# Joining the block scaling, moving the snapshot and q's transposes, and splitting the attention products in a linear-attention + FP4 block

## What is computed

```
xn = layernorm(x)
out = x + attention(xn) + ffn(xn)

attention:  q, k, v = split(xn @ W_qkv.T)        # 16 heads of 16
            q = softmax(q over the head's 16) / 4 ; k = exp(k)
            # tokens in buckets of 64; a bucket sees the sums of the buckets before it
            ksum    = exclusive cumsum over buckets of sum(k)
            context = exclusive cumsum over buckets of k^T v
            attn = (q context) / max(q . ksum, 1e-6)
            return attn @ W_out.T

ffn:        fp4_linear(a, w) = fq(a) @ fq(w).T
            # fq: blocks of 16 along the last dim, scale = max(|block|) / 6 (at least 1e-12),
            # each value to the nearest of 0, .5, 1, 1.5, 2, 3, 4, 6 times its scale
            h = silu(fp4_linear(xn, w_gate)) * fp4_linear(xn, w_up)      # 704 wide
            return fp4_linear(h, w_down)
```

## Time and profile before

| | |
|---|---|
| median of 3 runs | 1361.32 us (1359.19 to 1363.07) |
| the profiled execution | 1361.72 us, its span 1360.0 us |
| ACT busy | 969.4 us, 71% |
| POOL busy | 355.0 us, 26% |
| instructions | 41012 |
| granted TensorE clock, mean | 0.989 |
| HBM | 19.99 MB read, 16.78 MB written, 27 GB/s |

### The profile page before, as it was taken

One profiled execution on the slowest core, in us unless ns is written; L12 is line 12 of the kernel. 1 busy time (PEld: TensorE's weight loads), 2 busy tenths in 40 slices (PEclk: granted clock), 3 DMA queues, 4 the chain that ended last, 5 costly groups with the idle time before them and its releaser, 6 DMA issues.

```text
span 1360.0 us, 41012 instructions
## 1 busy us (share of the span) xinstructions
PE 1271.1 (93%) x9934; PEld 871.0 (64%) x9934; DVE 1309.7 (96%) x3901; ACT 969.4 (71%) x3221; POOL 355.0 (26%) x791
## 2 busy tenths in 40 slices
PE   0279999999999999999999999999999999999996
PEld 0157666666666666666666666666666666666664
DVE  6869999999999999999999999999999999999996
ACT  1567777777777777777777777777777777777772
POOL 2212223222222323222222222223232222323220
PEclk9889999999999999999999999999999999999998
DMA  4024544444454444444544444545454454445444
GB/s 129 12 40 82 108 98 100 105 100 102 98 114 100 101 105 98 103 100 98 113 101 105 98 102 99 112 98 104 105 109 99 92 115 101 96 105 110 97 83 91
DMA packets 432380, 133.64 MB, mean 98 GB/s; under 512 B 397404, under 2 KB 431836, under 8 KB 432348
## 3 DMA queue, kind: packets, MB, share of 16 engines
q1 hardware_dynamic: 431622, 132.60, 46.8%
q10 hardware_dynamic: 726, 0.72, 0.2%
HBM read 19.99 MB, written 16.78 MB: 27 GB/s over the span
## 4 chain that ended last, share of the span: by engine, by line
DVE 52%; issue 33%; DVEq 7%; PE 5%; ACT 2%; DMA 1%; SPq 0%; ACTq 0%
DVE hx_v L880 7%; DVE ga L810 5%; DVE blk L834 3%; DVE xring L963 3%; DVE hx_v L887 3%; DVE h L820 2%; DVE drec L794 2%; DVE xq_s L935 2%; DVE q_rows L922 2%; DVE att L799 2%; DVE osum L958 2%; DVE blk L843 1%; DVE dz L786 1%; DVE hrow L854 1%; DVE dmx L790 1%
## 5 line engine op out<-in xcount | busy, mean ns | idle before, releaser
L418 POOL TENSOR_TENSOR xn_s<-xn,xn_s 128x256 f16<-128x256 f32 x128 | 108.6, 848 | 820.3 <-ACT xn_s L535 820.3
L1165 PE MATMUL outp<-w_down_cat,q_rows 128*128 128x256 f16 x1408 | 246.1, 274 | 0.0
L617 ACT ACTIVATE snap<-ctxp,mask 64x68 f32<-64x68 f32 x1024 | 236.5, 310 | 3.3
L1165 PEld LDWEIGHTS outp<-w_down_cat,q_rows 128*128 128x128 f16 x1408 | 138.3, 98 | 16.5
L1167 PE MATMUL outp<-w_down_lo,q_rows 128*128 128x256 f16 x640 | 147.6, 274 | 0.0
L580 ACT ACTIVATE th<-unit0a,c_g 128x352 f32<-128x352 f32 x128 | 71.0, 554 | 97.3 <-PE unit0b L1078 95.3
L556 ACT ACTIVATE qexp<-qsh,c_q 128x256 f32<-128x256 f32 x128 | 65.1, 508 | 99.0 <-DVE qsh L773 98.8
L580 ACT ACTIVATE th<-unit1a,c_g 128x352 f32<-128x352 f32 x128 | 71.0, 555 | 87.4 <-PE unit1b L1078 65.0
L827 DVE TENSOR_REDUCE blk<-h 128x44 f32<-128x704 f32 x128 | 123.8, 967 | 0.1
L411 POOL TENSOR_TENSOR att_s<-att,att_s 128x256 f16<-128x256 f32 x128 | 87.9, 687 | 108.1 <-ACT att_s L572 108.1
L880 DVE TENSOR_TENSOR hx_v<-h,blk 128x704 f32<-128x704 f32 x128 | 111.0, 868 | 0.0
(11 more groups left out here) (199 smaller groups left out, 4059.0 us busy)
## 6 DMA issues: line engine op xcount, KB each, us to landing
xring<-x SPq DMA_DIRECT2D x128, 128.0 KB, 2.7
out<-xring SPq DMA_DIRECT2D x128, 128.0 KB, 2.5
xnt<-xn_s SPq DMA_TRANSPOSE x128, 2.5
xqt<-xq_s SPq DMA_TRANSPOSE x128, 2.4
att_t<-att_s SPq DMA_TRANSPOSE x128, 2.5
q_rows<-q_rows SPq DMA_TRANSPOSE x128, 3.6
raw_qkv<-wqkv_t SPq DMA_DIRECT2D x1, 768.0 KB, 4.4
raw_up<-wup ACTq DMA_DIRECT2D x2, 352.0 KB
```

The costliest lines, as they stand in the source:

```text
L418: nc.gpsimd.tensor_tensor(xn_s[:, par, 1, :], xn[:, par, :], xn_s[:, par, 0, :], ALU.subtract).then_inc(xn_lo, 1)
L617: nc.scalar.activation(kept[:, :, cols], sums[:, :, cols], ACT.Copy, scale=mask[rows, f, h:h + 1])\
L1165: nc.tensor.matmul(downp, hqt[:, par, m, :], w_down_cat[:, m, :], start=(m == 0), stop=False)
```

## The change

1. **Joined block scaling.** `block_scales` makes one instruction, `blk * SIX_TIE * 2^11` and the maximum with a tile `blk_floor` (60 columns, set once ahead of the loop), for h's 44 and x's 16 blocks. It waits for both maxima. A semaphore `blk_scaled` takes the place of one count each in `xq_step` (6 to 5 per tile) and `hq_step` (9 to 8).
2. **Snapshot between the tanh.** ACT runs `snapshot(k + 1)` right behind the first `tanh_gate`, and not as the last of the step. `squares_wait` stands ahead of `high_xn`, and `copy_qt` becomes ACT's last operation of the step.
3. **q's transposes last.** PE runs `transpose_q(k + 1)` at the end of the step, with a new wait for `att_step` of the tile before, that is for `attention(k)` of the same step to be over.
4. **Numerators.** Eight products of 64 rows of contraction and 72 columns, in place of four of 128 and 144. The halves `f` go to two banks: `nump` and `trp` are now the two halves of one tensor `pair`, and the numerators of `f = 1` lie in the bank of q's transposes, beside them.
5. **DVE's attention.** Reads go over both banks by one access pattern; the factor 4e-6 moves from the second part to the first; the product is two instructions of 128 elements, one for each `f`; it stands before `gate_h` of the second half, right behind the reciprocal.

The diff, cut to its core (counts of `xq_step` and `hq_step` that only shift are left out):

```
+        blk_floor = sb("blk_floor", [P, FB + XB])
...
-        nump = pb("nump")
+        pair = ctx.enter_context(nc.psum_tensor("pair", [P, 1024], fp32))
+        nump = pair[:, 0:512]
-        trp = pb("trp")
+        trp = pair[:, 512:1024]
+        nums = pair[:, :].rearrange("p (f x) -> p f x", f=2)[:, :, 2 * P:2 * P + HG * SW].rearrange("p f (g c) -> p g f c", c=SW)
...
                 tanh_gate(k, 0, par)
+                snapshot(k + 1)
                 normalise_waits(k + 3)
                 mean_waits(n, d + 4)
                 tanh_gate(k, 1, par)
                 factor_of_row(k - 1, odd)
                 normalise(n, d + 3)
                 mean_of(n, d + 4)
+                squares_wait(k + 4)
                 high_xn(k + 3, odd)
-                squares_wait(k + 4)
+                squares_of(n, d + 4)
                 copy_qt(k + 1, odd)
-                squares_of(n, d + 4)
-                snapshot(k + 1)
...
-                    nc.vector.tensor_copy(dz[:, :, :], num[:, :, CW:SW]).then_inc(att_step, 1)
+                    nc.vector.tensor_scalar(dz[:, :, :].rearrange("p (g f) h -> p g f h", f=2), nums[:, :, :, CW:SW], 4e-6, None, ALU.mult).then_inc(att_step, 1)
...
-                    nc.vector.scalar_tensor_tensor(dmx[:, :, :], dz[:, :, :], 4e-6, num[:, :, HD:CW:HE], ALU.mult,
-                                                   ALU.max).then_inc(att_step, 1)
+                    nc.vector.tensor_tensor(dmx[:, :, :].rearrange("p (g f) h -> p g f h", f=2),
+                                            dz[:, :, :].rearrange("p (g f) h -> p g f h", f=2),
+                                            nums[:, :, :, HD:CW:HE], ALU.max).then_inc(att_step, 1)
...
+                    for f in range(2):
+                        end = nc.vector.tensor_tensor(att[:, par, :].rearrange("p (g f h e) -> p f g h e", f=2, h=HH, e=HD)[:, f],
+                                                      nums[:, :, f, 0:CW].rearrange("p g (h e) -> p g h e", e=HE)[:, :, :, 0:HD],
+                                                      drec[:, :, :].rearrange("p (g f) (h o) -> p f g h o", f=2, o=1)[:, f]
+                                                      .broadcast_to([P, HG, HH, HD]), ALU.mult)
+                    end.then_inc(att_step, 1)
...
             def block_scales(t, u):
-                if is_tile(u):
-                    dve.wait_ge(xq_step, after(u, 6, 1))
-                    nc.vector.tensor_scalar(xblk[:, 1, :], xblk[:, 0, :], SIX_TIE * 2.0 ** 11, XS * TINY * 2.0 ** 11, ALU.mult, ALU.max)\
-                        .then_inc(xq_step, 1)
-                if is_tile(t):
-                    dve.wait_ge(hq_step, after(t, 9, 1))
-                    nc.vector.tensor_scalar(hblk[:, 1, :], hblk[:, 0, :], SIX_TIE * 2.0 ** 11, h_floor[:, :], ALU.mult, ALU.max)\
-                        .then_inc(hq_step, 1)
+                do_h, do_x = is_tile(t), is_tile(u)
+                if do_h:
+                    dve.wait_ge(hq_step, after(t, 8, 1))
+                if do_x:
+                    dve.wait_ge(xq_step, after(u, 5, 1))
+                if do_h or do_x:
+                    both = slice(0 if do_h else FB, FB + XB if do_x else FB)
+                    nc.vector.scalar_tensor_tensor(blk[:, 1, both], blk[:, 0, both], SIX_TIE * 2.0 ** 11, blk_floor[:, both],
+                                                   ALU.mult, ALU.max).then_inc(blk_scaled, 1)
...
                 attention(k, par, 2)
+                attention(k, par, 3)
                 gate_h(k, 1, par)
-                attention(k, par, 3)
                 times_up(k, 1, par)
...
                 pe.wait_ge(q_exp, after(t))
                 if begun(t - 1):
+                    pe.wait_ge(att_step, after(t - 1, 4))
+                if begun(t - 1):
                     pe.wait_ge(qt_done, after(t - 1))
...
+                pe.sem_inc(num_turn, 1)
                 for g in range(HG):
                     for s in range(2):
-                        rows = slice(s * BUCKET, (s + 1) * BUCKET)
-                        last = nc.tensor.matmul(nump[rows, g * 2 * SW:(g + 1) * 2 * SW],
-                                                qt[:, par, g * P + s * BUCKET:g * P + (s + 1) * BUCKET],
-                                                snap[:, g, s, :, :].rearrange("p f c -> p (f c)"), start=True, stop=True)
+                        for f in range(2):
+                            rows, cols = slice(s * BUCKET, (s + 1) * BUCKET), slice(f * VW, (f + 1) * VW)
+                            at = f * 512 + 2 * P + g * SW
+                            last = nc.tensor.matmul(pair[rows, at:at + SW],
+                                                    qt[cols, par, g * P + s * BUCKET:g * P + (s + 1) * BUCKET],
+                                                    snap[cols, g, s, f, :], start=True, stop=True)
...
                 gate_up(k, 1, par)
-                transpose_q(k + 1, odd)
                 project_att(k - 2, par)
                 project_h(k - 2, par)
+                transpose_q(k + 1, odd)
```

More of the change, by code:

```diff
@@ L203, in linear_attention_fp4_ffn_block @@
         num_done = sem("num_done")
+        num_turn = sem("num_turn")
         att_step = sem("att_step")
@@ L295, in turn_xq @@
                     return
-                sp.wait_ge(xq_step, after(t, 6))
+                sp.wait_ge(xq_step, after(t, 5))
                 sp.sem_inc(sp_turn, 1)
@@ L306, in turn_h @@
                     return
-                sp.wait_ge(hq_step, after(t, 9))
+                sp.wait_ge(hq_step, after(t, 8))
                 sp.sem_inc(sp_turn, 1)
@@ L520, in normalise_waits @@
                 if begun(t - 2):
-                    act.wait_ge(xq_step, after(t - 2, 6, 3))
+                    act.wait_ge(xq_step, after(t - 2, 5, 2))
             def normalise(n, d):
@@ L585, in scales_x @@
                     return
-                act.wait_ge(xq_step, after(t, 6, 2))
+                act.wait_ge(blk_scaled, t + 1)
                 nc.scalar.activation(xs_hi[:, :].rearrange("p (b i) -> p b i", i=2), twice(xblk[:, 1, :]), ACT.Copy)\
@@ L592, in factor_of_row @@
                     return
-                act.wait_ge(hq_step, after(t, 9, 4))
+                act.wait_ge(hq_step, after(t, 8, 3))
                 if begun(t - 2):
@@ L600, in scales_h @@
                     return
-                act.wait_ge(hq_step, after(t, 9, 5))
+                act.wait_ge(hq_step, after(t, 8, 4))
                 nc.scalar.activation(hs_hi[:, :].rearrange("p (b i) -> p b i", i=2), twice(hblk[:, 1, :]), ACT.Copy,
@@ L818, in times_up @@
                 if begun(t - 2):
-                    dve.wait_ge(hq_step, after(t - 2, 9, 6))
+                    dve.wait_ge(hq_step, after(t - 2, 8, 5))
                 nc.vector.tensor_tensor(h[:, par, half * FH:(half + 1) * FH], ga[:, half, :],
@@ L852, in over_one @@
                 if do_h:
-                    dve.wait_ge(hq_step, after(t, 9, 2))
+                    dve.wait_ge(blk_scaled, t + 4)
                     nc.vector.tensor_reduce(hrow[:, 0, :], hblk[:, 1, :], AX.X, ALU.max).then_inc(hq_step, 1)
@@ L856, in over_one @@
                     if do_x:
-                        dve.wait_ge(xq_step, after(u, 6, 2))
+                        dve.wait_ge(blk_scaled, u + 1)
                     both = slice(0 if do_h else FB, FB + XB if do_x else FB)
@@ L862, in row_scale @@
                 if is_tile(t):
-                    dve.wait_ge(hq_step, after(t, 9, 3))
+                    dve.wait_ge(hq_step, after(t, 8, 2))
                     if begun(t - 1):
@@ L871, in over_row @@
                     return
-                dve.wait_ge(hq_step, after(t, 9, 4))
+                dve.wait_ge(hq_step, after(t, 8, 3))
                 nc.vector.reciprocal(hrow[:, 2, :], hrow[:, 1, :]).then_inc(hq_step, 1)
@@ L920, in scale_h @@
                 else:
-                    dve.wait_ge(hq_step, after(t, 9, 7))
+                    dve.wait_ge(hq_step, after(t, 8, 6))
                 nc.vector.tensor_tensor(rows(hq_s[:, par, part * F:(part + 1) * F]), rows(hx_q[:, 0:F].bitcast(fp16)),
@@ L929, in scale_x @@
                 dve.wait_ge(hx_step, hx_after(t, 3))
-                dve.wait_ge(xq_step, after(t, 6, 4))
+                dve.wait_ge(xq_step, after(t, 5, 3))
                 if begun(t - 2):
@@ L1051, in _ @@
             low_cols()
-            dve.wait_ge(factors, 11)
+            dve.wait_ge(factors, 13)
             for n in range(0, 2):
```

17 lines of the change are left out of this document (8 added, 9 removed).

## The result

The changed kernel takes 1402.54 us (median of 5 runs, 1401.23 to 1403.29), the kernel before 1360.36 on the same chip (1359.19 to 1363.07): 1.0304 times the time, 95% interval 1.0291 to 1.0317. Over 120 steps of the middle a step grew from 9.907 to 10.248 us; 120 times 0.341 is 40.9 us, near the 39.9 us by which the span grew (1360.0 to 1399.9).

The account below looks back on a forecast made before the run. The prediction took a loop through PE, ACT, POOL and DVE as the bound; two steps of 19.65 + N, N = 0.7, give 10.18 us a step, +0.30 over some 121 steps, +36 on 1361.7: 1398 us, range 1366 to 1420.

Parts of the forecast that it names:

- the loop through ACT and POOL: PE's products release ACT's tanh, ACT releases POOL, whose subtraction holds DVE's scaling: 10.18 us a step, +0.30; chance 0.56.
- DVE's own list: DVE's work in a step without holds: 9.68 + 0.24 + 0.06 - 0.02 = 9.96 us.
- The bound of the kernel before: A loop through all engines at 9.885 us a step; DVE's own work 9.68, PE without waits 9.75.
- Begins at the same place: The joined scaling starts where L847 did, behind L827's end; unblocked it saves 0.02 us, and POOL can hold it.
- DVE's order: Product behind reciprocal, times_up behind gate_h: two back-to-back dependences, +0.24 us a step, and +0.06 for the split product.
- N: Length of PE's numerators stage with sixteen instructions: taken as 0.7 us, bounds 0.4 (half the columns' time) to 1.06.
- A: Start of the first half of DVE's attention product L799, from which the loop's times are counted.
- rival 1: POOL is through before DVE's scaling asks; DVE's own work sets 9.96 us a step, 1371 us; chance 0.18.
- the long scaling: Sign on DVE: the joined scaling's mean well above 0.25 us, its ends coinciding with those of POOL's L411.
- None ahead of the output projection: Sign on PE: idle ahead of the transposes on the attention product, but none ahead of L1074's output projection.
- rival 2: Products of different rows run beside each other (N = 0.4) and chained DVE instructions cost nothing: 1346 us; chance 0.11.
- Rival 3: PE's new products cost time: N above 1.06, PE sets the step with 9.30 + N; at 1.25, 1442 us; chance 0.06.

Follow-up runs that it names:

- The first experiment: The changed kernel with the two waits ahead of the joined scaling exchanged, x's maximum first and h's last: 1390.11 us, ratio 1.0207 to the kernel before.

## Why the prediction was right, and where it wasn't

The forecast was 1398 us, the range 1366 to 1420, and the time 1402.5. The number is good, but what I named as the pace isn't it: two misses cancelled, and that they did is luck. The forecast had the loop through ACT and POOL at 10.18 a step and DVE's own list at 9.96 behind it. The loop came out lower, some 10.03, and DVE's list higher, 10.25, and the step is the higher of the two.

**The bound of the kernel before** was read rightly. DVE's own 9.68 showed as 9.682 once POOL's work was taken away. PE's 9.75 was no floor, since its transposes' stage gave 0.07 back: in the kernel before that stage is 0.44 in the mean and 0.22 at least, so the 0.29 of the step that I read held 0.07 of waiting.

**The joined scaling.** "Begins at the same place" failed, by 0.11: L834 to L855 is 1.110, where it was L827 to L843 0.884 and some 0.11 to L847. The rows of the dependence were of an instruction with one wait; the new one has two, the late one first. The first experiment shows it, and so do two more kernels: 1.106 with the joined scaling alone, 0.998 with x's wait first and the snapshot moved. What I said of the rest holds: the joined form can be held by POOL as L847 was (392 ns with the old order in the changed kernel, 347 where the snapshot's move is the only other part), as the Trainium skill (SBUF — State Buffer, "Who interferes with whom") has it.

**DVE's order** was +0.30 forecast and is +0.358. Both new dependences have the price taken from the earlier trace rows: the reciprocal to the product is 0.277 for 0.163 to what stood there before, L817 to L827 0.544 for 0.43. The two halves take 0.406 for the forecast 0.40 (0.33 before; that is +0.07, where the sum had +0.06). The 0.05 that I missed is L817's length: behind the reciprocal it took 0.46 (0.377 to the next start, plus 0.08), and in its new place 0.51, as the other `gate_h` of a step always did. The Trainium skill (VectorE: DVE Perf Modes, "The DRAIN you can't avoid") has a chain of copies with a semaphore behind each take no longer than one without. If that meant that a wait for the instruction in front is free, 0.277 for 0.163 says that here it isn't.

**The loop's turn** wasn't in the sum at all: +0.108. Before, times_up overlapped the instruction in front, and with the turn it took 0.54 to the next start for 0.43 without. Now it is 0.75 for 0.44. That the branch is what costs is shown by the kernel with half the turns; that it costs more because times_up itself starts late, as it waits for `ga`, is argued. The kernel before with the order alone has the same 0.75, so it comes from the order.

DVE's list by these: 9.96 + 0.11 + 0.06 + 0.108 = 10.24, measured 10.25.

**The products.** N is 0.41, the end of my bounds that I hadn't taken (half the columns' time, 0.4): sixteen products at 0.026 us each. As a term of the loop that is 0.29 too much in two steps, 0.15 a step; at N = 0.41 the loop gives 10.03, 1379 us. The context's stage grew by 0.05. No run has the new products alone, so this is read from the trace; with DVE's list as the pace, what they save PE doesn't show in the time.

**The loop through ACT and POOL** was followed well. With A = 738.57, gate_up is at A + 3.89 (forecast 3.93 with this N), L416 ends 5.02 behind the second tanh (5.03) and at A + 13.26 (13.39). From the A of the next step, where the projection begins 0.3 later behind the transposes, gate_up is at A + 4.22 and L416 ends at A + 13.61; the mean of the two is 0.04 above the forecast. It doesn't set the pace because DVE asks later: at A + 13.66 in either step, where the unheld DVE of the forecast, at A + 9.96 + 3.06 = A + 13.02, would have been there ahead of both ends, and held. This is rival 1, POOL through before the scaling asks, at a price that my own list, 9.96, had too low; its condition came about mainly by DVE being 0.64 late, and less by POOL being early (0.25 ahead of the 13.68 that N = 0.7 gave). The two limits lie close together: with the waits exchanged, at 10.14 a step, L416 ends 0.12 to 0.13 behind the scaling's start in every other step and doesn't hold it yet; at 0.28, in the old order of the changed kernel, it does (0.36 for 0.22). And with that old order the loop is the pace, at the same 10.25.

**Of what would show it**: L805 0.285 and twice, the second tanh directly behind the snapshot, POOL's small operations directly followed by L416 (740.57 and 740.72), PE waiting ahead of the transposes: all there. Not there are the long scaling and its ends together with those of POOL's subtraction. L817 and L827 are 0.54 apart, not 0.50. The scaling's mean is 229 ns, which I had named as the sign of rival 1. "None ahead of the output projection" failed: PE still waits there for L971, 119 times.

**Rivals 2 and 3.** The first half of rival 2 has its number, N = 0.41 for 0.4, the second failed: the dependences cost what the rows said. The 0.41 agrees with what the Trainium skill says of different tiles, that they work in parallel (TensorEngine Tiling, "Key Properties"); that this is the reason no run here shows. Rival 3 fell with N. In the working PE alone is 9.30 + N in one place and 9.35 + N in another; nothing hangs on it.

## What to carry to other kernels

When an instruction gets a second wait, put the wait that is met last also last in the program: here the other order cost 0.11 us a step. Write down for each new dependence between neighbours of a full engine what it costs (0.11 here), and look at what stands behind the last instruction of a loop. Where POOL and DVE hold each other, an edit of 0.1 us can decide which of them is held, so a single part, right in itself, can cost more than all of them together: time the parts in the combination that you mean to keep.

## What the runs showed that I had not expected

- Two waits ahead of one DVE instruction: 0.147 us behind the end of its input with the late one first, 0.035 with it last.
- Sixteen fp32 instructions of 64 rows, 64 columns of weights and 72 columns take 0.41 us; the eight of 128 rows and 144 columns took 0.54.
- With POOL's subtraction recorded 0.03 us ahead of DVE's instruction of two inputs, POOL is the one held (1.08 for 0.67 us); 0.08 and 0.09 ahead, DVE is (0.96 for 0.52). Between 0.05 and 0.06 the kernel before has both. Taking these holds away gains 27 us of 1361.
- A record of the joined scaling that overlaps the end of POOL's by 0.12 us is no longer than others (0.22 us); at 0.28 it is 0.36, at 0.38 it is 0.46.
- One order of two DVE instructions, with nothing else changed, cost 105 us, 83 of it in holds at other places than the one where it was made.
- DVE's turn of the loop costs 0.31 us (0.75 for 0.44) where its last instruction starts behind its neighbour's end, and 0.11 where it overlaps it.
